# A twelve-sublayer decoder on one core: the quantised feed-forward and the gated experts, each as one stage over all batch elements

## The reference, cut to what matters

```python
def act_quant(x):                     # per token
    scale = 127.0 / jnp.clip(jnp.max(jnp.abs(x), axis=-1, keepdims=True), 1e-05)
    return jnp.clip(jnp.round(x * scale), -128, 127) / scale
def weight_quant(w):                  # one scale per matrix
    scale = 1.0 / jnp.clip(jnp.mean(jnp.abs(w)), 1e-05)
    return jnp.clip(jnp.round(w * scale), -1, 1) / scale
h = act_quant(x) @ weight_quant(w1).T              # 128 -> 512
h = depthwise_conv1d(h, conv_w, conv_b)            # 3 taps along the tokens
y = act_quant(silu(h)) @ weight_quant(w2).T        # 512 -> 128
```

```python
shared_y = (silu(x @ sw1.T) * (x @ sw3.T)) @ sw2.T           # 128 -> 256 -> 128
scores = softmax(x @ Wg.T); vals, ids = top_k(scores, 2); w = vals / vals.sum()
y = shared_y + sum(combine[:, e] * ((silu(x @ W1[e].T) * (x @ W3[e].T)) @ W2[e].T) for e in range(8))
```

## Time and profile before

| | us |
|---|---|
| median of 3 runs | 5654.67 (5646.64 to 5674.03) |
| the profiled execution itself | 5665.67 |
| its span | 5663.4 |
| L2f, first to last instruction ahead of its normalisation | 4495.0 to 4725.4 |
| L3f, the same | 5345.3 to 5642.6 |

### The profile page before, as it was taken

The page is one execution under the profiler, slowest core; times in us unless marked ns, Lnnn a source line. Parts: engine busy times, 40 slices in busy tenths (PEclk is TensorE's granted clock), DMA queues, the critical chain, the costliest instruction groups (busy, mean ns, idle before and its releaser), DMA issues. The chain is left out here.

```text
span 5663.4 us, 100659 instructions
## 1 busy us (share of the span) xinstructions
PE 4616.4 (82%) x36210; PEld 2809.5 (50%) x36210; DVE 3167.7 (56%) x6182; ACT 2854.6 (50%) x8728; POOL 1976.5 (35%) x2119
## 2 busy tenths in 40 slices
PE   3998779997988979889798899655589736888888
PEld 1665346565655646646466465344466522224433
DVE  6452245455756747567476575399945554654333
ACT  2452234455756747667476574477724312543411
POOL 0230000136939839579396692033213200000000
PEclk6999979899999999999999998767689856997888
DMA  0000000001111111111112111000000000001000
GB/s 32 22 1 4 15 11 7 17 2 27 45 40 41 45 42 44 44 37 45 37 45 55 31 45 34 19 1 1 1 5 1 4 0 7 9 3 34 3 0 8
DMA packets 34488, 122.26 MB, mean 22 GB/s; under 512 B 8484, under 2 KB 9512, under 8 KB 32424
## 3 DMA queue, kind: packets, MB, share of 16 engines
q1 hardware_dynamic: 33960, 115.44, 7.6%
HBM read 36.45 MB, written 1.05 MB: 7 GB/s over the span
## 5 line engine op out<-in xcount | busy, mean ns | idle before, releaser
L640 POOL MEMSET norm_eps<- 128x1 f32 x16 | 1.6, 98 | 1920.0 <-POOLq L116 1861.0
L2095 POOL TENSOR_TENSOR local_other<-local_raw,local_sin 128x256 f32<-128x256 f32 x768 | 557.3, 726 | 60.2
L1956 PE MATMUL ps<-arena,local_xs 128*128 128x512 f32 x768 | 440.3, 658 | 109.5 <-DVE local_raw L2136 60.4
L2092 POOL TENSOR_TENSOR local_rot<-local_raw,local_cos 128x512 f32<-128x512 f32 x384 | 488.2, 1271 | 68.3 <-DVE local_raw L2136 68.2
L2098 POOL TENSOR_TENSOR local_rot<-local_rot,local_other 128x512 f32<-128x512 f32 x384 | 486.6, 1267 | 30.1
L2069 ACT ACTIVATE ps<-ps,local_negmax 128x96 f32<-128x96 f32 x1536 | 474.2, 309 | 41.0 <-DVE local_negmax L2130 41.0
L2136 DVE SCALAR_TENSOR_TENSOR local_raw<-local_inverse,ps 128x512 f32<-128x512 f32 x384 | 264.1, 688 | 274.1 <-ACT local_inverse L2063 274.1
L2126 DVE TENSOR_REDUCE local_norm<-local_squares 128x8 f32<-128x512 f32 x384 | 263.2, 685 | 133.6 <-ACT local_squares L2038 133.6
L2069 ACT ACTIVATION_READ_ACCUMULATOR ps<-ps,local_negmax 128x1 f32 x1536 | 309.8, 202 | 0.0
L2038 ACT ACTIVATE local_squares<-ps 128x512 f32<-128x512 f32 x384 | 229.8, 598 | 158.5 <-PE ps L1956 158.3
L2001 PE MATMUL ps<-const,local_probs 128*96 128x128 f32 x1536 | 237.0, 276 | 75.7 <-DVE local_probs L2154 75.7
(11 more groups left out here) (510 smaller groups left out, 11083.9 us busy)
## 6 DMA issues: line engine op xcount, KB each, us to landing
local_V_span<-local_V SPq DMA_DIRECT2D x96, 384.0 KB, 4.0
local_V_span<-local_V SPq DMA_DIRECT2D x96, 256.0 KB, 3.6
arena<-in_L1f_a SPq DMA_DIRECT2D x7, 2176.0 KB, 8.3
local_V_span<-local_V SPq DMA_DIRECT2D x72, 128.0 KB, 2.3
arena<-in_L3f SPq DMA_DIRECT2D x1, 3460.0 KB, 11.3
arena<-in_L1f_f SPq DMA_DIRECT2D x6, 537.5 KB, 3.9
arena<-in_L0f SPq DMA_DIRECT2D x1, 2824.5 KB, 9.9
arena<-in_L0x SPq DMA_DIRECT2D x1, 2049.5 KB, 9.1
```

Source lines behind the costliest of these rows:

```text
L1956: nc.tensor.matmul(bank("qk", n)[:, :], tokens_of(tile), w("Wqkv", QKV[i] * 512, (QKV[i] + 1) * 512), start=True, stop=True)\
L2092: link(nc.gpsimd.tensor_tensor(rot, raw, m.cos[:, t, a * DH:(a + 1) * DH].unsqueeze(1) .broadcast_to([P, 8, DH]), ALU.mult))
L2095: link(nc.gpsimd.tensor_tensor(other[:, :, lo:lo + HALF], raw[:, :, HALF - lo:DH - lo], m.sin[:, t, a * DH + lo:a * DH + lo + HALF].unsque ...
```

## The change

Both sublayers become one stage each for all four elements, so that there is no barrier between steps or elements.

`bit_ffn_all`: the weights are quantised once, not once per element. The convolution is no longer done by DVE: w1 (quantised) is multiplied by each of the three tap rows, and the hidden features come from three accumulating matmuls per chunk, each against the quantised x shifted by one token (x_quant has a zero column at either end). SiLU on ACT reads PSUM and adds the convolution's bias. The quantisation's small steps (scale and reciprocal) work on four tiles at once. The elements are shifted against one another: in step s PE makes the hidden features of element s, turns them, and then turns back and projects element s-1. `turn_x` and `back_x` are four transpositions each, `read_x` an ACT copy; `whole` are the quantised weights, `z` the hidden features after SiLU, `rows` their quantised tiles, `quant` those turned back. The weights of L2f grow by `conv_rows`, 3 x 512 columns per partition.

`experts_all`: 8 units (2 chunks x 4 elements) of the shared expert run first, with the routing of all 16 token tiles on DVE between them; then 64 units of the experts. The share of an expert is no longer multiplied into the hidden chunks but into x (`scaled`), which feeds the W3 product; it is spread for two experts at a time by two matmuls with 32 rows each, on different rows of the array (partitions 0 to 31 and 32 to 63). A unit is two products into one of two (before: three) pairs of banks, and its W2 product follows two units later.

```diff
+def bit_ffn_all(core, _, arena):
...
+    TURNED, RING, ROWS, OUT = core.ps[0:4], core.ps[4:6], core.ps[6], core.ps[7]
+    uses = []
+    for s in range(B + 1):
+        uses += [("hidden", s, m) for m in range(M) if s < B] + [("back", s - 1, c) for c in range(M) if s >= 1]
+    place = {use: RING[n % 2] for n, use in enumerate(uses)}
+    held = {use: uses[n - 2] for n, use in enumerate(uses) if n >= 2}
...
+            def convolve(b, m):
+                wait_bank(("hidden", b, m))
+                pe.wait_ge(x_read, b + 1)
+                for j in range(TAPS):
+                    mm = nc.tensor.matmul(place["hidden", b, m][:, :], taps[:, j, m * P:(m + 1) * P],
+                                          x_quant[:, b % 2, j:j + S], start=(j == 0), stop=(j == TAPS - 1))
+                mm.then_inc(hidden_ready, 1)
+
+            def turn_hidden(b):
+                pe.wait_ge(hidden_read, M * (b + 1))
+                for t in range(QT):
+                    if b >= 1:
+                        pe.wait_ge(tile_read, QT * (b - 1) + t + 1)
+                    for c in range(M):
+                        mm = nc.tensor.transpose(TURNED[t][:, c * P:(c + 1) * P], z[:, c, t * P:(t + 1) * P], core.ident)
+                    mm.then_inc(turned, 1)
...
+                pe.wait_ge(rows_ready, QT * (b + 1))
+                for t in range(QT):
+                    mm = nc.tensor.transpose(place["back", b, c][:, t * P:(t + 1) * P],
+                                             rows[:, b % 2, t, c * P:(c + 1) * P], core.ident)
+                mm.then_inc(back_ready, 1)
+
+            def project(b, c):
+                if c == 0 and b >= 1:
+                    pe.wait_ge(stored, b)
+                pe.wait_ge(back_read, M * b + c + 1)
...
+            turn_x(0)
+            pe.wait_ge(sums_ready, 2)
+            nc.tensor.matmul(OUT[:, 0:2], core.c("ones"), sums[:, :], start=True, stop=True).then_inc(total_ready, 1)
+            back_x(0)
+            turn_x(1)
+            pe.wait_ge(edges, 2)
+            pe.wait_ge(taps_ready, TAPS)
+            for s in range(B + 1):
+                if s < B:
+                    for m in range(M):
+                        convolve(s, m)
+                        if m == 1 and s >= 1 and s + 1 < B:
+                            turn_x(s + 1)
+                    turn_hidden(s)
+                if s >= 1:
+                    if s == 1:
+                        pe.wait_ge(second_ready, 1)
+                    back_hidden(s - 1, 0)
+                    back_hidden(s - 1, 1)
+                    for c in range(M):
+                        if c + 2 < M:
+                            back_hidden(s - 1, c + 2)
+                        project(s - 1, c)
+                if s + 1 < B:
+                    back_x(s + 1)
...
+                if s >= 1:
+                    for c in range(M):
+                        act.wait_ge(back_ready, M * (s - 1) + c + 1)
+                        if c == 0 and s >= 2:
+                            act.wait_ge(projected, s - 1)
+                        nc.scalar.copy(quant[:, c, :], place["back", s - 1, c][:, :]).then_inc(back_read, 1)
+                    act.wait_ge(projected, s)
+                    nc.scalar.copy(core.sums[:, s - 1, :], OUT[:, :]).then_inc(stored, 1)
+                if s + 1 < B:
+                    read_x(s + 1)
...
+            def quantize_hidden(b):
+                for t in range(QT):
+                    dve.wait_ge(turned, QT * b + t + 1)
+                    link(nc.vector.tensor_reduce(top[:, t:t + 1], TURNED[t][:, :], AX_X, ALU.max,
+                                                 apply_absolute_value=True))
+                scales()
+                for t in range(QT):
+                    here, one = rows[:, b % 2, t, :], slice(t, t + 1)
+                    nc.vector.tensor_scalar(here, TURNED[t][:, :], scale[:, one], ROUND, ALU.mult, ALU.add)\
+                      .then_inc(tile_read, 1)
+                    dve.wait_ge(tile_read, QT * b + t + 1)
+                    link(nc.vector.tensor_scalar(here, here, ROUND, 127.0, ALU.subtract, ALU.min))
+                    nc.vector.tensor_scalar(here, here, -128.0, unit[:, one], ALU.max, ALU.mult).then_inc(rows_ready, 1)
...
+            quantize_x(0)
...
+            quantize_weights(0)
+            for j in range(TAPS):
+                nc.vector.tensor_tensor(taps[:, j, :], whole[:, 0, :], w("conv_rows", j * 512, (j + 1) * 512), ALU.mult)\
+                  .then_inc(taps_ready, 1)
+            quantize_x(1)
+            quantize_weights(1)
+            for b in range(B):
+                quantize_hidden(b)
+                if b + 2 < B:
+                    quantize_x(b + 2)
+    residual_norm_all(core, core.sums)
...
+SPREAD_LEAD, SHARED_UNITS = 3, 2 * B
...
+            def products(g):
+                b = element(g)
+                if g >= 2:
+                    pe.wait_ge(gated_ready, g - 1)
+                cols = slice(chunk(g) * P, (chunk(g) + 1) * P)
+                nc.tensor.matmul(product(g, 0)[:, :], w("W1", cols.start, cols.stop), tokens_of(core, b), start=True,
+                                 stop=True)
+                if g < SHARED_UNITS:
+                    rhs = tokens_of(core, b)
+                else:
+                    e = b * EXPERTS + offset(g) // OWN
+                    if offset(g) % OWN == 0:
+                        pe.wait_ge(scaled_ready, e + 1)
+                    rhs = scaled[:, e % 4, :]
+                nc.tensor.matmul(product(g, 1)[:, :], w("W3", cols.start, cols.stop), rhs, start=True, stop=True)\
+                  .then_inc(products_ready, 1)
...
+            def spread_pair(p):
+                b, q = divmod(p, EXPERTS // 2)
+                pe.wait_ge(turned_read, b + 1 + (q == EXPERTS // 2 - 1 and b + 1 < B))
+                if p >= 1:
+                    pe.wait_ge(scaled_ready, 2 * p)
+                for r in range(2):
+                    rows, e = slice(32 * r, 32 * r + 32), 32 * r + 2 * q + r
+                    mm = nc.tensor.matmul(SPREAD[r][:, :], core.ident[rows, e:e + 1].broadcast_to([32, P]),
+                                          shareT[rows, b % 2, :], start=True, stop=True)
+                mm.then_inc(spread, 1)
...
+            for t in range(TILES):
+                mm = nc.tensor.matmul(LOGITS[:, t * 8:(t + 1) * 8], tokens_of(core, t // QT)[:, t % QT * P:(t % QT + 1) * P],
+                                      w("Wg"), start=True, stop=True)
+            mm.then_inc(logits_ready, 1)
+            for g in range(SHARED_UNITS):
+                products(g)
+            turn_shares(0)
+            pe.wait_ge(logits_read, 1)
+            for b in range(2):
+                project_shared(b)
+            spread_pair(0)
+            for g in range(SHARED_UNITS, UNITS):
+                b, o = element(g), offset(g)
+                products(g)
+                if o == 7 and b + 1 < B:
+                    turn_shares(b + 1)
+                if o == 2 and b >= 2:
+                    project_shared(b)
+                before = g - 2
+                if before >= SHARED_UNITS:
+                    project(before, False, offset(before) == EACH - 1)
+                if (o + SPREAD_LEAD) % 4 == 0 and (g - SHARED_UNITS + SPREAD_LEAD) // 4 < PAIRS:
+                    spread_pair((g - SHARED_UNITS + SPREAD_LEAD) // 4)
+            pe.wait_ge(gated_ready, UNITS)
+            for g in (UNITS - 2, UNITS - 1):
+                project(g, False, g == UNITS - 1)
...
+            def scaling(p):
+                dve.wait_ge(spread, p + 1)
+                b = p // (EXPERTS // 2)
+                for r in range(2):
+                    nc.vector.tensor_tensor(scaled[:, 2 * (p % 2) + r, :], tokens_of(core, b), SPREAD[r][:, :], ALU.mult)\
+                      .then_inc(scaled_ready, 1)
...
+            largest(range(0, 6))
+            gating(0)
+            largest(range(6, 12))
+            gating(1)
+            largest(range(12, TILES))
+            nc.vector.tensor_tensor(share[:, :, :], logits[:, :, :], best[:, :, 0:1].broadcast_to([P, TILES, 8]),
+                                    ALU.subtract).then_inc(arg_ready, 1)
+            gating(2)
+            places(range(0, 6))
+            gating(3)
+            places(range(6, 12))
+            gating(4)
+            places(range(12, TILES))
...
+            scaling(0)
+            for g in range(SHARED_UNITS, UNITS):
+                gating(g)
+                p = (g - SHARED_UNITS + 2) // 4
+                if offset(g) % 4 == 2 and p < PAIRS:
+                    scaling(p)
+    residual_norm_all(core, core.sums)
 
...
-             ("L2f", each(bit_ffn)), ("L3a", projected_attention), ("L3x", cross_narrow), ("L3f", each(experts))]
+             ("L2f", bit_ffn_all), ("L3a", projected_attention), ("L3x", cross_narrow), ("L3f", experts_all)]
...
+    p.add("conv_rows", np.tile(x["L2_ffn_conv_w"][:, 0, :].T.reshape(1, -1), (P, 1)))
```

(46 more changed lines are left out.)

314 lines of the change are left out of this document (161 added, 153 removed).

## The result

The changed kernel took 5464.43 us (median; 5452.07 to 5482.79), the kernel before beside it 5659.44: ratio 0.9657, 95% interval 0.9619 to 0.9696. The prediction was 5438 (5410 to 5480).

The account below looks back on a forecast made before the run. L2f was taken as bound by the engines' sum, L3f by PE, partly at half clock. Gains of 131 and 85 us made 216, from 5665.7 to 5449, or 5438 against typical runs; range 5410 to 5480.

Parts of the forecast that it names:

- L2f's sum: Quantised feed-forward: start, four shifted steps and end add up to 99 us instead of 230.4, a gain of 131.
- What I called the next bound: L2f steps: DVE has 4.8 us to spare, so ACT's copies are late next, not DVE.
- the 3.2 set aside for the clock there: End of L2f: 3.2 us added in case the clock falls while PE waits for DVE's last hidden tiles.
- The clock in L2f: Rival, chance 0.20: clock falls in every L2f step, costing 5 us a step, 20 in all: 5458.
- My "against": Argument against the clock falling in L2f: transpositions among matmuls run at 0.43 us per four.
- L3f's sum: Experts stage: PE's products, spreads and waits add up to 212.5 us against 297.3, a gain of 84.8.
- The expert units begin at 25.3: Start of L3f: logits, shared units, waits, two projections and first spread end 25.3 us into the stage.
- a pair is 0.96: L3f: two 32-row spreads on different rows overlap, 0.96 us a pair; fifteen further pairs make 14.4.
- The serial spreads: Rival, chance 0.10: L3f's paired spreads do not overlap, 1.72 us a pair, 12 us more: 5450.
- Two banks: Rival, chance 0.06: in L3f a late gate or scale holds PE, 16 us in all: 5454.
- The half clock: Rival, chance 0.02: TensorE stays at 1.2 GHz through both stages, slower than before: 5720.
- From stages to the run: Whole kernel: stage gains of 131 and 85 make 216 us, giving 5438; later attention stages allowed 15 either way.

Follow-up runs that it names:

- e8: Changed kernel with L3f's logits behind two shared units, x's turn-backs and copy earlier, needless warming products in L2f: 5460.04 us, ratio 0.9664 to the kernel before.
- e7: Changed kernel with the 16 transpositions of the hidden tiles in each L2f step done four times over: L2f 117.0 us.
- e5: Changed kernel with L3f's 16 logit products behind the first two shared units and those units' gates ahead of the routing: L3f 219.8 us, 219.85 without the edit.
- e10: Changed kernel with each pair of spreads in L3f done six times over: L3f 288.5 us.
- e6: Changed kernel with both spreads of a pair on the same rows, 0 to 31: L3f 235.1 us, 15.3 longer.
- e11: Kernel before with spreads on 128 rows instead of 8 and five needless products per element covering the routing: L3f 282.1 us.
- e12: Kernel before with spreads on 128 rows instead of 8, without needless products: L3f 287.6 us.
- the halves: Kernel before with only L2f changed, then with only L3f changed: 5525.70 us (ratio 0.9766) and 5573.21 us (ratio 0.9861).
- e4: Kernel before with five needless 128x512 products in each element's routing: 5676.95 us, L3f from 297.5 to 285.9.
- e9: Changed kernel without edits, measured a second time against the kernel before: 5445.76 us, ratio 0.9623.

## Why the prediction held, step by step

- **L2f's sum.** Predicted 99, measured 98.5. Its terms: tap products begin at 9.8 (10.4), the products of element 1 at 27.2 (26.4), steps of 20.62 (20.4), the last turn-backs 22.4 after their step's start (22.1). What I called the next bound, ACT's copies and not DVE, shows as the 0.78, 0.24 and 0.82; taking away the wait for the copy of x in e8 gave 0.9 a step. Part of the 0.5 us of agreement is luck, since errors cancel: step 0 was 1.4 longer than laid out (its 24 passes took 13.45, not 12.2), the start 0.6 shorter, and the time from the last turn-backs to the end 7.7 instead of 9.7, as the 3.2 set aside for the clock there were too many.
- **The clock in L2f** (rival, 0.20). The windows view has it at 1.00 from 4521 to 4590, over three and a half steps:

```profile
4521.00:4590.00 69.00, 61.51 (x237) 33.15 (x235) 46.23 (x111) 19.67 (x32) 0.00 (x0) 1.00 0.00 0
```

  and e7 shows why the rival fails: even 7 us of transpositions don't bring it down. My "against", the 0.43 per four, pointed the right way.
- **L3f's sum.** Predicted 212.5, measured 219.6. Two terms were too small. "The expert units begin at 25.3": they began at 28.85. I had the logits at full clock and no fall behind them; the three products behind them lost 2.5 us at half clock, the logits 0.4, and the rest is spread over small steps. The waits before units 5, 6 and 7 came to 2.7, as laid out. e5 shows that moving the logits doesn't bring the 2.5 back, since the clock falls behind them there too. And "a pair is 0.96": a group is 11.55 instead of 11.28, so a pair costs 11.55 - 10.32 = 1.23, 0.27 more; 15 x 0.27 = 4.1. e10 shows that 0.86 of it is the two spreads and 0.37 the step into and out of a lone pair.
- **The serial spreads** (rival, 0.10). e6: wrong, and it would have cost 14, not 12.
- **Two banks** (0.06). From the first expert unit on PE's timeline has one wait for a gate, 0.56 us before the last two projections, and PE is busy 216.1 of 219.6 us. **The half clock** (0.02) misread: it was the eight rows and the pause (e11, e12), not spreads as such (e10).
- **From stages to the run.** Predicted gain 216; measured 195 in the first measurement, 212 in the second, 211 as the sum of the halves. The stages give 209.6: 7 us of L3f less than predicted, 1 of L2f more. In the first pair of profiles 14.5 more were lost in stages that the change leaves alone: 10.6 in L0x and L1a, which stand ahead of it, 4.6 in L3a, 3.3 in L3x, less some 4 elsewhere. Of these only the 4 or so of L3a are handed on by the new L2f; I had them at nothing. That the second measurement came within 8 us of my 5438 is in part the luck of this spread.

## What to carry to other kernels

Lay out a pipeline instruction by instruction from the trace's own durations, and look for the short waits on the third engine: the forecast of L2f came within 1 us in that way, no single term of it being off by more than 2. Judge an edit of a few us by the length of its own stage in the trace, and then by the stage behind it: e8 won 6 us in L2f and paid 6 in the normalisation and the attention that follow. Two 32-row matmuls on different 32-row parts of the array cost 0.86 us in a row of such pairs, as one 128-row product does, and 1.23 as a lone pair between such products.

## What the runs showed of the hardware that I had not expected

- Between wide products, transpositions of 128x128 float32 hold the clock at 1.00: 64 in a row, 0.110 us each (e7). So do 32-row matmuls in pairs, 24 passes in a row (e10, 1.00 over 260 us).
- Matmuls on 8 rows didn't: clock 0.69 with PE busy 10.10 of 10.10 us, where 128 rows have 1.00 with PE busy 7.10 of 7.10 (e4, e11). So a busy share of 100% in the profile doesn't mean full clock.
- Shorter work in one stage can move the fall of the clock into the next: the same normalisation took 17.2 us at 0.99 in e9 and 21.2 at 0.68 in e8.
- The same instructions of an unchanged stage took 120 us at 0.50 in one execution and 79 at 0.85 in another (L3x of e11 and e12).
